# Second layer's feed forward over tokens sorted by routed expert: 17 blocks with one routed expert each, in place of 16 batches with both

## Chip, cores, metric

One core of one Trainium2 chip. The metric is the device time of one execution in microseconds (us). The kernel before takes 2658.98 us, the median of three runs (2656.93 to 2663.84).

## What is computed

Sixteen sequences of 256 tokens with 256 features go through two layers. Each layer is cross attention with 16 heads and then a feed forward, both added to the residual with a tanh gate. The change touches the feed forward of the second layer only:

```python
def _L1_ffn_ref(x, gate_w, w1, b1, w2, b2, sw1, sb1, sw2, sb2):
    xf = x.reshape(-1, D)                      # layer-normed tokens
    gate_scores = xf @ gate_w.T                # two routed experts
    top1 = jnp.argmax(softmax(gate_scores), axis=-1)
    one_hot = jax.nn.one_hot(top1, 2)
    masked = xf[None, :, :] * one_hot.T[:, :, None]
    h = relu(einsum('end,edh->enh', masked, w1) + b1[:, None, :])
    expert_out = einsum('enh,ehd->end', h, w2) + b2[:, None, :]
    shared = relu(xf @ sw1 + sb1) @ sw2 + sb2
    return expert_out.sum(axis=0) + shared     # hidden size 1024
```

An expert that is not chosen for a token still adds `relu(b1) @ w2 + b2`, the same vector for every token. All arithmetic is float32. Layer projections are made as three float32r products of high and low parts (`product3`).

## The kernel before

The program is written engine by engine; nothing schedules it. `layer0` is untouched by the change. `layer1` (from about 1357 us of the span) runs over batches of 256 tokens, two tiles of 128. Every engine has a function `body`, and one iteration of it is a software pipeline: batch `a` is in attention, batch `b = a - 1` in the feed forward, batch `c = a - 2` (on DVE) in its last sum, and `nxt = a + 1` has its first projections made. Inside, 20 steps `s` interleave the work of one head of attention with one piece of the feed forward. The order of each engine's instructions is fixed by this code, and engines wait for each other by semaphores.

Attention, per head and step: PE makes the scores of two heads (`pair_scores`, lines 1512 to 1524, even steps), DVE the row maximum (L1367), ACT the exponential (L1268), DVE the reciprocal (L1372), POOL the normalisation (L1157), PE the transposes (L1535, three steps later), DVE their copy (L1379), PE the product with the values (L1546 to L1549). The score tiles have two PSUM banks, so the pair of step `s + 2` starts when ACT has read both of step `s`. Projections of the own batch stand at steps 0 to 3 (v0, v1, k1, q1), of the next at 9, 14 and 16. After the steps PE makes `attn_out` (L1560) and DVE the residual (`attn_final`, L1385 and L1389).

Feed forward of batch `b`: DVE `ffn_norm` (L1299 to L1339) normalises, makes the two gate scores and `x0`, the tokens of expert 0 with the others zero; PE transposes `xf` and `x0` (L1488); ACT takes the high part, DVE the low (L1320); POOL makes `x1T = xfT - x0T` (L1172). Twelve hidden groups of 12 matmuls each follow, one per step at steps 0 to 11: four of the shared expert on `xfT`, four of expert 0 on `x0T`, four of expert 1 on `x1T`. ACT applies bias and relu (L1242). `ffn_down` (L1572) sums 24 chunks of hidden features for each token tile: tile 0 at the steps 16 to 19, tile 1 after `attn_out`. A float32 matmul of 128x256 counts as two instructions in the trace. DVE adds the biases (L1396) and the residual (L1403), and SP stores.

SP's loop (L1122) loads the input and the context of batch `b`, stores `b - 2`, and loads the residual of `b`. The load of the next batch waits only for `xn_ready` and `ctx_ready` of the batch before.

The weights of the feed forward are split into high and low parts once, in two pieces of 3072 columns, at steps 4 and 8 of iteration 0 (ACT L1206, DVE L1453). The head of DVE's body and the end of PE's:

```python
def body(a, b, c, nxt):
    if b is not None:
        ffn_norm(b)
    if c is not None:
        ffn_final(c)
...
def body(a, b, nxt):
...
    if a is not None:
        attn_out(a)
    if b is not None:
        for piece in range(4):
            ffn_down(b, 1, piece)
```

## Times and profile before

| | us |
|---|---|
| median of 3 runs | 2658.98 |
| lowest, highest | 2656.93, 2663.84 |
| the profiled execution's own time | 2655.57 |
| its span, first to last instruction | 2653.8 |
| PE busy | 2302.0 (87%) |
| DVE, ACT, POOL busy | 1493.3, 1267.8, 1022.9 |
| mean granted TensorE clock | 0.958 of 2.4 GHz |

The page gives the busy time of each engine over the span, slices, the chain that ended last, and the costliest groups of instructions. Matmuls overlap: one of 128x256 is shown as 280 to 380 ns long, while the next starts 117 ns later (float32r) or 216 ns later (one of the two instructions of a float32 product). So lengths of stretches are read from the starts, not from the sum of busy times.

### The profile page before, as it was taken

How to read it: one execution, taken by the hardware profiler on the slowest of the kernel's cores; microseconds unless marked ns; L12 is line 12 of the kernel's file. 1: busy time of each engine (PE TensorE's matmuls, PEld its weight loads, DVE VectorE, ACT ScalarE, POOL GpSimd, SP SyncE). 2: the span in 40 equal slices, each digit the busy share in tenths (PEclk: the TensorE clock that was granted, in tenths of full speed). 3: DMA queues.
4: the chain of work that ended last, by engine and by line, in shares of the span. 5: the costliest groups of instructions: out<-in, count | busy, mean ns of one | idle time of the engine just before them, and what ended most of it. 6: DMA issues, size and time to landing. Idle time of an engine off the chain costs nothing. (4 is left out here: it accounts for less than half of the span.)

```text
span 2653.8 us, 48232 instructions
## 1 busy us (share of the span) xinstructions
PE 2302.0 (87%) x16128; PEld 1929.3 (73%) x16128; DVE 1493.3 (56%) x3906; ACT 1267.8 (48%) x3971; POOL 1022.9 (39%) x910
## 2 busy tenths in 40 slices
PE   5888888888888888888456999999999999999998
PEld 4667777777777777776344777877777887777777
DVE  3467667676766776767645445444444544444441
ACT  5655566555556555556023444433344443334441
POOL 1355564555554555555512333221233322123320
PEclk8999999999989999999677999999999999999999
DMA  4000000000000000000040000000000000000000
GB/s 145 14 6 17 13 16 4 16 16 16 16 12 4 16 16 16 16 4 9 4 161 1 13 17 16 16 16 16 4 12 16 16 16 16 16 4 12 16 9 9
DMA packets 25856, 51.66 MB, mean 19 GB/s; under 512 B 6272, under 2 KB 7040, under 8 KB 24640
## 3 DMA queue, kind: packets, MB, share of 16 engines
q1 hardware_dynamic: 25792, 50.84, 5.7%
q8 instruction: 37, 0.61, 0.1%
q14 instruction: 27, 0.22, 0.0%
HBM read 42.44 MB, written 8.39 MB: 19 GB/s over the span
## 5 line engine op out<-in xcount | busy, mean ns | idle before, releaser
L1157 POOL TENSOR_SCALAR l_probs<-l_probs,l_rinv 128x256 f32<-128x256 f32 x512 | 238.9, 482 | 587.0 <-DVE l_rinv L1372 585.3
L1268 ACT ACTIVATE l_probs<-l_score,l_negmax 128x256 f32<-128x256 f32 x512 | 238.9, 473 | 264.6 <-DVE l_negmax L1367 264.6
L335 POOL TENSOR_TENSOR l_prod<-l_att,l_kv 128x2048 f32<-128x2048 f32 x64 | 288.3, 4545 | 181.2 <-DVE l_att L608 181.2
L321 POOL TENSOR_TENSOR l_prod<-l_q,l_kv 128x2048 f32<-128x2048 f32 x64 | 290.3, 4548 | 151.7 <-DVE l_att L591 80.8
L1572 PE MATMUL l_ffn<-l_w,l_hid 128*128 128x256 f32 x1536 | 347.1, 381 | 1.0 <-ACT l_hid L1242 1.0
L1572 PEld LDWEIGHTS l_ffn<-l_w,l_hid 128*128 128x128 f32 x1536 | 287.0, 190 | 50.1 <-issue 13.5
L1379 DVE COPY l_probsT<-l_attn 128x512 f32<-128x512 f32 x256 | 175.4, 685 | 157.6 <-PE l_attn L1535 157.3
L681 DVE CUSTOM_DVE_ANT_0 l_probs<-l_score,l_mbias 128x256 f32<-128x256 f32 (+1 forms) x512 | 161.2, 352 | 140.2 <-PE l_score L877 91.8
L1367 DVE TENSOR_REDUCE l_negmax<-l_score 128x2 f32<-128x512 f32 x256 | 174.9, 683 | 64.4 <-PE l_score L1523 64.4
L614 DVE TENSOR_REDUCE l_h<-l_prod 128x128 f32<-128x2048 f32 x64 | 146.3, 2286 | 103.4 <-POOL l_prod L335 102.4
L427 ACT COPY l_probsT<-l_attn 128x384 f32<-128x384 f32 x256 | 121.1, 473 | 143.8 <-PE l_attn L887 143.8
L410 ACT ACTIVATE l_probs<-l_probs,l_negmax 128x256 f32<-128x256 f32 x256 | 130.9, 511 | 104.4 <-DVE l_negmax L681 104.4
L110 PE MATMUL l_moe<-l_we_hi,l_h2T_hi 128*128 128x256 f32 x512 | 160.1, 313 | 12.4 <-DVE l_acc L665 10.7
L1242 ACT ACTIVATE l_hid<-l_ffn,l_b 128x256 f32<-128x256 f32 x384 | 161.5, 478 | 11.9 <-PE l_ffn L112 10.1
L1535 PE MATMUL l_attn<-l_ident,l_probs 128*128 128x128 f32 x1024 | 154.9, 277 | 9.4 <-DVE l_probsT L1379 7.3
L875 PE MATMUL l_score<-l_kT,l_qT 64*128 64x256 f32 x256 | 98.2, 467 | 61.2 <-DVE l_negmax L681 61.2
L110 PE MATMUL l_attn<-l_cT_hi,l_wk_hi 128*128 128x256 f32 x384 | 122.8, 320 | 31.8 <-DVE l_xT_lo L545 31.8
L591 DVE TENSOR_REDUCE l_att<-l_prod 128x128 f32<-128x2048 f32 x64 | 145.9, 2279 | 5.8 <-issue 3.9
L111 PE MATMUL l_moe<-l_we_lo,l_h2T_hi 128*128 128x256 f32 x512 | 147.9, 289 | 0.0
L112 PE MATMUL l_moe<-l_we_hi,l_h2T_lo 128*128 128x256 f32 x512 | 147.7, 289 | 0.0
L1535 PEld LDWEIGHTS l_attn<-l_ident,l_probs 128*128 128x128 f32 x1024 | 118.7, 142 | 23.6 <-issue 10.0
L665 DVE SCALAR_TENSOR_TENSOR l_acc<-l_moe,l_gate,l_acc 128x256 f32<-128x256 f32 x256 | 110.7, 474 | 40.8 <-PE l_moe L112 26.7
(273 smaller groups left out, 7441.9 us busy)
## 6 DMA issues: line engine op xcount, KB each, us to landing
l_ctxin<-in_ctx SPq DMA_DIRECT2D x32, 256.0 KB, 3.0
l_xin<-in_x SPq DMA_DIRECT2D x16, 256.0 KB, 2.7
l_x<-in_x SPq DMA_DIRECT2D x16, 256.0 KB, 2.6
x<-l_acc SPq DMA_DIRECT2D x16, 256.0 KB, 2.0
l_xin<-x SPq DMA_DIRECT2D x16, 256.0 KB, 3.3
l_x<-x SPq DMA_DIRECT2D x16, 256.0 KB, 2.7
out<-l_x SPq DMA_DIRECT2D x16, 256.0 KB, 2.0
l_hid<-in_w SPq DMA_DIRECT2D x2, 1536.0 KB, 9.7
```

What stands on the lines that cost most here:

```text
L110: last = nc.tensor.matmul(out, wh, xh, start=n == 0, stop=False)
L111: last = nc.tensor.matmul(out, wh, xl, start=False, stop=False)
L321: nc.gpsimd.tensor_tensor(prod[:, u].rearrange("p (h g d) -> p h g d", h=half, g=H), q4[:, u * half:(u + 1) * half].unsqueeze(2).to_broadc ...
L335: nc.gpsimd.tensor_tensor(prod[:, u].rearrange("p (h d g) -> p h d g", h=half, d=HD), a4.unsqueeze(2).to_broadcast([P, half, HD, H]), v4.u ...
L681: last = V.tensor_tensor_reduce(out=probs[:, j % 4, lo:hi], in0=ps[:, lo:hi], in1=mbias[:, lo:hi], scale=-HD0 ** -0.5, scalar=3e38, op0=AL ...
L1157: last = nc.gpsimd.tensor_scalar(probs[:, j % 4, t * S:(t + 1) * S], probs[:, j % 4, t * S:(t + 1) * S], rinv[:, j, t:t + 1], 1.0, ALU.mul ...
L1242: last = nc.scalar.activation(hid[:, c, :], ps[:, u * S:(u + 1) * S], ACT.Relu, bias=b1[:, c:c + 1])
L1268: last = nc.scalar.activation(probs[:, s % 4, t * S:(t + 1) * S], ps[:, t * S:(t + 1) * S], ACT.Exp, bias=negmax[:, s, t:t + 1], accum_out ...
L1367: V.tensor_reduce(negmax[:, j], ps[:].rearrange("p (t k) -> p t k", t=NT), axis=AX.X, op=ALU.max, negate=True).then_inc(max_ready, 1)
L1379: V.tensor_copy(probsT[:, j % 3, :], ps[:]).then_inc(free, 1)
L1535: last = T.transpose(ps[:, kt * S + t * P:kt * S + (t + 1) * P], probs[:, j % 4, t * S + kt * P:t * S + (kt + 1) * P], ident[:])
L1572: last = T.matmul(ps[:, 0:D], hid[:, c, t * P:(t + 1) * P], w2[:, c, :], start=c == 0, stop=c == 3 * NHC - 1)
```

## The change

The routed experts no longer see every batch. Each batch, after attention, is only routed: DVE makes the gate scores, PE ranks the tokens of expert 0 within the batch by a product with a triangle of ones, DVE forms for each token a place in the DRAM tensor `slots` (expert 0 from the front, expert 1 from the back), and POOL writes the 256 rows there by two indirect DMAs. A row holds the 256 features, the token's number, its mean and its reciprocal deviation. The feed forward then runs over 17 blocks of 256 rows of `slots`. Each block belongs to one routed expert, which DVE chooses from the counts (`choose`) and SP reads into registers. The weights of that expert come from DRAM for each block: the two split parts `e1` (1 MB each), the bias `be`, the second weights `e2` (1 MB), and `ce`, the constant of the expert not chosen. The output is written token by token, by two indirect DMAs of POOL for each block. A 17th block is needed because the places of the two experts need not end on a multiple of 256. Unused places are filled once with rows that go to rows of the output behind the last token.

A block has 8 hidden groups and 16 chunks in place of 12 and 24. The feed forward lags attention by three batches in place of one, so that three iterations have attention alone (0, 1, 2), thirteen have both (3 to 15), and four have the feed forward alone (blocks 13 to 16). Before it was one, fifteen and one.

```diff
+        hidden_at = {0: 0, 3: 1, 4: 2, 5: 3, 6: 4, 7: 5, 8: 6, 9: 7}
+        down_at = {10 + n: (2 * n, 2 * n + 2) for n in range(8)}
+        split_at = {4: 3, 8: 4, 14: 5}
-        ffn = Banks(nc, ctx, "l1_ffn", ["xfT", "x0T"] + [f"h{j}" for j in range(12)] + ["y0", "y1"])
+        ffn = Banks(nc, ctx, "l1_ffn", ["xfT"] + [f"h{j}" for j in range(8)] + ["y"])
...
@@ SP
+                def load_block(d):
+
+                    wait_apart(sp, sp_passed, choice_ready, d + 1)
+                    e = sp.value_load(choice[0:1, 0:1], min_val=0, max_val=1)
+                    n = sp.value_load(choice[0:1, 1:2], min_val=0, max_val=NBLOCK - 1)
...
+                        wait_apart(sp, sp_passed, scattered, 32 * (d + 2))
+                    if not first(d):
+                        wait_apart(sp, sp_passed, xe_copied, d)
+                    sp.dma_start(xe[:], slots.rearrange("(k t p) n -> k p t n", t=NT, p=P)[bass.ds(n, 1)][0]).then_inc(xe_in, 16)
...
+                        _, _, emptied, turn = ffn.at("h3", d - 1)
+                        wait_apart(sp, sp_passed, emptied, turn + 1)
+                    for part in range(2):
+                        sp.dma_start(flat(e1[part]).bitcast(F32), e1_parts[bass.ds(e, 1), part][0]).then_inc(e1_in, 16)
+                    sp.dma_start(be[:], ins["b1"][:, bass.ds(e * NHC + NHC, NHC)]).then_inc(e1_in, 16)
+                def load_second(d, e):
...
+                        wait_apart(sp, sp_passed, x4_ready, d)
+                    sp.dma_start(flat(e2), ins["w2"][:, bass.ds(e * (NHC * D) + NHC * D, NHC * D)]).then_inc(e2_in, 16)
+                    sp.dma_start(ce[:], ce_parts[bass.ds(e, 1)][0]).then_inc(e2_in, 16)
-                with sp.Fori(2, B) as b:
-                    load(b)
-                    store(b - 2)
-                    load_residual(b)
+                def body(i, d, nxt):
+                    if d is not None:
+                        e = load_block(d)
+                    if i is not None:
+                        load_residual(i)
+                    if nxt is not None:
+                        load(nxt)
+                    if d is not None:
+                        load_second(d, e)
+                with sp.Fori(3, B - 1) as i:
+                    body(i, i - 2, i + 1)
...
@@ POOL
+                def body(a, r, f, nxt):
+                    if f is not None and not first(f):
+                        store(f - 1)
+                    if r is not None:
+                        power(varF_ready, rstdF_ready, varF, rstdF, r)
                     for j in range(H):
...
+                        if r is not None and j == 3:
+                            scatter(r)
                         if nxt is not None and j == 5:
                             split_context(nxt)
...
@@ DVE
+                def place(r):
+                    dve.wait_ge(rank_ready, r + 1)
...
+                    V.tensor_tensor(count0[:], ranks[:, NT:NT + 1], count0[:], ALU.add).then_inc(rank_read, 1)
+                def other_expert():
+                    dve.wait_ge(split_lo, NS)
+                    V.tensor_scalar(b1[:, NHC:3 * NHC], b1[:, NHC:3 * NHC], 0.0, None, ALU.max)
+                    V.tensor_copy(hid[:, :, 0:P], b1[:, NHC:3 * NHC].unsqueeze(2).to_broadcast([P, 2 * NHC, P])).then_inc(relu_ready, 1)
+                    dve.wait_ge(other_full, 1)
...
+                def body(a, r, d, f, done, nxt):
+                    if r is not None:
+                        dve.drain()
+                        variance(x3, statF, mvF, varF, varF_ready)
+                    if done is not None:
+                        ffn_final(done)
+                    if f is not None:
+                        low(ffn, "xfT", f, xfT, xfT_hi)
+                    if r is not None:
+                        route(r)
                     for s in range(STEPS):
...
+                        if r is not None and s == 2:
+                            place(r)
+                        if d is not None and s == 2:
+                            choose(d)
...
+                        if d is not None and s == 15:
+                            block_normalise(d)
...
@@ PE
+                def rank(r, f):
+                    pe.wait_ge(wins_ready, r + 1)
+                    T.matmul(ps[:, 0:NT], above[:], first_wins[:], start=True, stop=False)
+                    T.matmul(ps[:, 1:NT], ones[:], first_wins[:, 0:1], start=False, stop=True)
+                    T.matmul(ps[:, NT:NT + 1], ones[:], first_wins[:, 0:1], start=True, stop=False)
+                    T.matmul(ps[:, NT:NT + 1], ones[:], first_wins[:, 1:2], start=False, stop=True).then_inc(rank_ready, 1)
+                def other_expert():
+                    pe.wait_ge(relu_ready, 1)
+                    pe.wait_ge(e2_raw_in, 32)
+                    for e in range(2):
+                        for c in range(NHC):
+                            last = T.matmul(ps[:, e * D:(e + 1) * D], hid[:, e * NHC + c, 0:P], (e2, w2)[e][:, c, :], start=c == 0, stop=c == NHC - 1)
                 def body(a, r, f, nxt):
...
+                        if r is not None and s == 2:
+                            rank(r, f)
+                        if f is not None:
+                            if s in hidden_at:
+                                if hidden_at[s] == 1 and r is not None:
+                                    pe.wait_ge(rank_read, r + 1)
+                                ffn_up(f, hidden_at[s])
+                            if s in down_at:
+                                ffn_down(f, 0, *down_at[s])
...
+                    if f is not None:
+                        ffn_down(f, 1, 0, 2 * NHC)
                     if a is not None:
                         attn_out(a)
-                    if b is not None:
-                        for piece in range(4):
-                            ffn_down(b, 1, piece)
```

In `store(f)` and `scatter(r)` POOL waits for `x4_ready` or `slot_ready` and issues one `indirect_dma_start` for each of the two tiles. The rank products go into the PSUM bank of the hidden group `h1`.

Three places of the order. First DVE, from the statistics of the batch that has left attention to the first row maximum of the next one. Before:

```order
L1304 TENSOR_SCALAR l_varF<-l_mvF 128x2
L1328 TENSOR_SCALAR l_xf<-l_x,l_mvF,l_rstdF 128x256 [waits l1_rstdF_ready]
...
L1336 TENSOR_TENSOR l_first_wins<-l_gscore 128x2
L1339 TENSOR_SCALAR l_x<-l_xf,l_first_wins 128x256 x2
...
L1396 TENSOR_TENSOR l_x<-l_ffn,l_b2sum 128x256 [waits l1_ffn1_full]
...
L1403 SCALAR_TENSOR_TENSOR l_x<-l_x,l_tg,l_x3res 128x512 [waits l1_x3_copied]
L1320 TENSOR_TENSOR l_xfT_lo<-l_ffn,l_xfT_hi 128x512 [waits l1_xfT_hi]
L1320 TENSOR_TENSOR l_x0T_lo<-l_ffn,l_x0T_hi 128x512 [waits l1_x0T_hi]
...
L1367 TENSOR_REDUCE l_negmax<-l_score 128x2 [waits l1_score0_full]
```

Now:

```order
L1409 TENSOR_SCALAR l_varF<-l_mvF 128x2
...
L1559 TENSOR_TENSOR l_x<-l_ffn,l_ce 128x512 [waits l1_stored]
L1563 CAST l_dest<-l_x3res 128x2 [waits l1_xe_copied]
L1564 SCALAR_TENSOR_TENSOR l_x<-l_x,l_tg,l_x3res 128x512
...
L1425 TENSOR_TENSOR l_xfT_lo<-l_ffn,l_xfT_hi 128x512 [waits l1_xfT_hi]
L1431 TENSOR_SCALAR l_xg<-l_row,l_mvF,l_rstdF 128x256 [waits l1_rstdF_ready]
...
L1442 TENSOR_TENSOR l_first_wins<-l_gscore 128x2
L1444 TENSOR_SCALAR l_other<-l_first_wins 128x2
L1446 TENSOR_TENSOR l_other<-l_other,l_down 128x2
...
L1527 TENSOR_REDUCE l_negmax<-l_score 128x2 [waits l1_score0_full]
```

The last sum of the feed forward (`ffn_final`) moved ahead of the gate scores, and the gate scores of the next batch now stand between the low part and the first maximum. Second, POOL at the head of the loop, now:

```order
L1265 DMA out<-l_x,l_dest 4352x256 [waits l1_x4_ready]
L1265 DMA out<-l_x,l_dest 4352x256
L1229 TENSOR_TENSOR l_rstdF<-l_varF,l_neghalf 128x2 [waits l1_varF_ready]
```

Before, the reciprocal deviation (`l_rstdF`, L1142) stood first and no store was POOL's. Third, SP's loop, now:

```order
L1137 DMA l_xe<-slots 128x2x260
...
L1145 ISA [waits l1_ffn0_free]
L1145 DMA l_e_hi<-e_parts 128x2048
...
L1145 DMA l_e_lo<-e_parts 128x2048
...
L1146 DMA l_be<-in_b 128x8
...
L1123 DMA l_row<-x 128x2x256
...
L1112 DMA l_xin<-x 128x512
L1115 DMA l_ctxin<-in_ctx 128x512 [waits l1_ctx_ready]
```

The loads of the next batch's input and context stand behind the wait for the fourth hidden group (`l1_ffn0_free`) and behind 2 MB of weights; before they stood at the head of the loop.

## Rows read from the trace of the kernel before

**Rows 1.** The page, costliest groups: ACT's exponential.

```profile
L1268 ACT ACTIVATE l_probs<-l_score,l_negmax 128x256 f32<-128x256 f32 x512 | 238.9, 473 | 264.6 <-DVE l_negmax L1367 264.6
```

**Rows 2.** Stretch, us; busy (count) PE, PEld, DVE, ACT, POOL; clock; DMA share; GB/s.

```profile
1372.00:1382.00 10.00, 5.83 (x38) 5.35 (x37) 4.90 (x11) 4.56 (x13) 0.00 (x0) 0.84 1.00 390
1379.00:1443.00 64.00, 41.21 (x272) 29.50 (x272) 35.35 (x68) 27.68 (x81) 17.43 (x35) 0.81 0.18 75
1444.00:1458.00 14.00, 8.27 (x40) 7.71 (x41) 6.88 (x24) 3.03 (x8) 0.70 (x1) 0.52 0.01 2
1597.00:1674.00 77.00, 72.66 (x520) 60.72 (x519) 36.23 (x90) 32.45 (x105) 21.11 (x39) 1.00 0.04 14
2598.00:2654.00 56.00, 49.48 (x297) 44.74 (x295) 9.58 (x27) 11.25 (x26) 3.84 (x4) 0.99 0.03 10
```

**Rows 3.** One line's instructions: the residual after attention; ns min/median/max, first and last start.

```profile
L1389 DVE SCALAR_TENSOR_TENSOR l_x<-l_ytmp,l_tg,l_x x16: 750/752/753, 1442.9 to 2598.9; 128x512 f32<-128x512 f32 x16
```

**Rows 4.** Timeline of PE, transposes and products: start us, us, engine, [idle before <-releaser].

```profile
1449.43 0.87 PE L1488 MATMUL l_ffn<-l_ident,l_xf 128*128 128x128 f32 x3 [7.30 <-DVE l_x L1339]
...
1670.08 3.69 PE L1560 MATMUL l_attn<-l_wo,l_oT 128*128 128x256 f32 x16 [0.76 <-issue]
...
2629.08 20.96 PE L1572 MATMUL l_ffn<-l_w,l_hid 128*128 128x256 f32 x96 [1.02 <-ACT l_hid L1242]
```

**Rows 5.** Timeline of ACT in the last feed forward: one hidden group.

```profile
2614.09 0.84 ACT L1242 ACTIVATE l_hid<-l_ffn,l_b 128x256 f32<-128x256 f32 x2 [0.56 <-PE l_ffn L112]
```

**Rows 6.** Timeline of DVE, end of one iteration and head of the next.

```profile
1676.67 0.17 DVE L1304 TENSOR_SCALAR l_varF<-l_mvF 128x2 f32<-128x2 f32 x1
1677.65 0.73 DVE L1328 TENSOR_SCALAR l_xf<-l_x,l_mvF,l_rstdF 128x256 f32<-128x256 f32 x2 [0.82 <-POOL l_rstdF L1142]
...
1680.05 0.16 DVE L1336 TENSOR_TENSOR l_first_wins<-l_gscore 128x2 f32<-128x2 f32 x1
...
1684.75 0.75 DVE L1403 SCALAR_TENSOR_TENSOR l_x<-l_x,l_tg,l_x3res 128x512 f32<-128x512 f32 x1 [0.16 <-issue]
1685.42 0.68 DVE L1320 TENSOR_TENSOR l_xfT_lo<-l_ffn,l_xfT_hi 128x512 fp32r<-128x512 f32 x1
...
1686.62 0.68 DVE L1367 TENSOR_REDUCE l_negmax<-l_score 128x2 f32<-128x512 f32 x1
```

**Rows 7.** Timeline of PE, head of the next iteration.

```profile
1683.97 0.60 PE L1488 MATMUL l_ffn<-l_ident,l_xf 128*128 128x128 f32 x4
...
1686.81 0.36 PE L110 MATMUL l_ffn<-l_xfT_hi,l_w_hi 128*128 128x256 f32 x1 [0.84 <-DVE l_x0T_lo L1320]
...
1691.43 0.35 PE L1521 MATMUL l_score<-l_k_hi,l_q 32*128 32x256 f32 x1
```

**Rows 8.** Timeline of POOL: reciprocal deviation, context split, normalisation.

```profile
1676.92 0.70 POOL L1142 TENSOR_TENSOR l_rstdF<-l_varF,l_neghalf 128x2 f32<-128x2 f32 x1 [20.18 <-DVE l_varF L1304]
...
1630.30 0.63 POOL L1149 CAST l_cT_hi<-l_ctxin 128x512 fp32r<-128x512 f32 x1
1631.09 1.28 POOL L1151 TENSOR_TENSOR l_cT_lo<-l_ctxin,l_cT_hi 128x512 fp32r<-128x512 f32 x1 [0.15 <-issue]
1632.35 0.93 POOL L1157 TENSOR_SCALAR l_probs<-l_probs,l_rinv 128x256 f32<-128x256 f32 x2
```

**Rows 9.** Timeline of DVE, steps 2, 3 and 7 of a full iteration.

```profile
1618.77 0.87 DVE L1347 SCALAR_TENSOR_TENSOR l_k_lo<-l_attn,l_bk,l_k_hi 128x256 fp32r<-128x256 f32 x2 [3.12 <-ACT l_k_hi L1230]
...
1633.07 0.74 DVE L1299 BATCH_NORM_STATS2 l_statC<-l_xin 128x6 f32<-128x256 f32 x2
```

**Rows 10.** Timeline of PE, scores of steps 2 and 4 in that iteration.

```profile
1614.14 0.35 PE L1521 MATMUL l_score<-l_k_hi,l_q 32*128 32x256 f32 x1
...
1621.44 0.35 PE L1521 MATMUL l_score<-l_k_hi,l_q 32*128 32x256 f32 x1
```

**Rows 11.** Timeline of SP: the next batch's input is asked for.

```profile
1618.22 0.33 SPq L1091 DMA_DIRECT2D l_xin<-x  x1
```

**Rows 12.** Timeline of DVE, a weight split in iteration 0.

```profile
1396.28 3.36 DVE L1453 TENSOR_TENSOR l_w_lo<-l_hid,l_w_hi 128x3072 fp32r<-128x3072 f32 x1 [3.07 <-ACT l_w_hi L1206]
```

More of the change, by code:

```diff
@@ L1096, in load_residual @@
                 def load_residual(b):
-                    if not first(b):
-                        sp.wait_ge(x3_copied, b)
-                        sp.wait_ge(xf_ready, b)
-                    sp.dma_start(x3[:], x2[bass.ds(b, 1)][0]).then_inc(xres_in, 16)
-                def store(b):
-                    sp.wait_ge(x4_ready, b + 1)
-                    sp.dma_start(out[bass.ds(b, 1)][0], x4[:]).then_inc(x4_stored, 16)
+                    if first(b):
+                        sp.wait_ge(gap_stored, 32)
+                    else:
+                        sp.wait_ge(scattered, 32 * b)
```

376 lines of the change are left out of this document (244 added, 132 removed).

## Prediction

> **What bounds the kernel now.** I read the busy time by stretch first. In a full iteration of the second layer PE has 72.66 us of records in 77, DVE 36.23, ACT 32.45, POOL 21.11, and the DMA engines move 14 GB/s at a share of 0.04 [rows 2]. So PE bounds it, at full clock. The residual after attention starts sixteen times between 1442.9 and 2598.9 us [rows 3], one iteration per 77.07 us, and 54.9 us follow the last. Second, what may take PE's place: an iteration with attention alone. Iteration 0 is one. From its first scores to its end, 64 us, PE has 41.21 us and the granted clock averages 0.81 [rows 2]. Heads pass in turn through DVE, ACT, POOL and PE, and less work on PE doesn't shorten that round. So less feed forward is worth what a full iteration loses until that round binds, less what the new iterations cost.
>
> **What PE loses.** A hidden group passes every 1.40 us (ACT's 0.84 and the 0.56 before it, waiting for PE) [rows 5]: four fewer, 5.6 us. The last feed forward's 96 instructions take 20.96 us, 0.437 for each of 48 float32 products [rows 4]: 16 fewer, 7.0. One set of transposes fewer, 0.6 [rows 7]; the rank products add some 0.5 (an estimate from the cheapest groups here). Net 12.7 us per iteration. POOL loses the two subtractions of `other_tokens`, as long as the 1.28 of the context's [rows 8], DVE a low part of 0.68 [rows 6]; neither engine bounds.
>
> **The head of an iteration.** Call T the end of the output product, near 1673.6 in the rows [rows 4]. Before, DVE's first maximum starts at 1686.62, T + 13.0 [rows 6], but PE fills this with the second half of `ffn_down`, 24 products or 10.4 us, and transposes. Now that half stands ahead of the output product and covers nothing. DVE's chain: variance done at 1676.84, T + 3.2 [rows 6]; then the last sum and residual, two passes of 0.68 and 0.75 with 0.2 between, so `x4_ready` at T + 5.0; low part to T + 5.7. POOL waits for `x4_ready`, issues two indirect DMAs and only then makes the reciprocal deviation, 0.70 [rows 8]. No row shows an indirect DMA. Bounds for one: 0.33, what SP needs to issue a DMA [rows 11], and 4.5, some three and a half of POOL's 1.28 us passes over 128x512 [rows 8], since it handles 128 rows one by one. I take 1.2, near POOL's pass over such a tile. The deviation is then there at T + 8.3. From there to the gate's comparison it is 2.40 (1677.65 to 1680.05) [rows 6], and three copies and three small operations with drains make 1.0. First maximum at T + 11.7. The next pair of scores needs maximum 0.68, two exponentials of two passes of 0.473 [rows 1], relu 0.84 between them [rows 5], hand-overs: 3.6. The scores of step 2 start at T + 15.3; before at 1691.43, T + 17.8 [rows 7]. PE has 4 us of work in this stretch, so of 10.4 + 0.6 + 1.4 us that left it, only 2.5 are gained.
>
> The Trainium skill, "DMA: Bandwidth & Descriptors", section "Anatomy of one DMA — SWDGE (gpsimd) path", gives about 2.0 us plus bytes / 436e9 per DMA from GpSimd, most of it the receipt and not the issue. By it two DMAs would be done 2.3 us after issue, and if POOL were held as long for each, the head would be 2.2 us longer than in my sum. No row here shows which.
>
> **Steps 2 to 4.** Before, 1614.14 to 1621.44: 7.3 us with two hidden groups in it [rows 10]. Now `h1` waits for `rank_read`. DVE gives it in `place`, which stands behind the low part of k1, and that waits 3.12 us for ACT behind PE's k1 projection [rows 9]. Scores, rank and k1 take PE 2.7; ACT 0.9; DVE's low part 0.87 [rows 9]; `place` 0.5: PE stands some 2.4 us. Then come two more operations of `place` and eight of `choose`, 0.16 each with five drains, 1.8, ahead of the maximum of step 3; 0.68 and an exponential of 1.0 later step 4 can score: 8.8 us. The queue behind also makes the next maximum 0.6 late.
>
> **Steps 4 to 10.** SP asks for the next batch's input at 1618.22 now, 15 us before DVE's use at 1633.07 [rows 9, 11]. After the change it does so behind the wait for the fourth hidden group, step 5, whose relu ends near T + 31, and behind 2 MB of `e1` and two smaller loads. At the 390 GB/s that the start of the layer reached [rows 2] 2 MB take 5.4 us, the 0.75 MB with them 2.0, landing and issues 2: the input is there at T + 40, the context a little later. DVE wants the one at step 7, T + 36; POOL the other after head 5 and needs 2.0 us with it before it can normalise head 6 [rows 8]. I take 4 us of stall; bounds 0 (loads that share the queue and finish early) and 7. The rest stays as in the trace of the same iteration, read off the starts of the scores: 11.8 us for steps 4 to 8 and 7.1 for 8 to 10.
>
> **Steps 10 to the end.** With less beside them steps 10 to 12 fall to 4.4 and 12 to 14 rise to 4.6, since a pair with no feed forward beside it takes 4.1 (steps 12 to 14 of that iteration). From step 14 to T: 23.6 before; 8.7 us of products go and 6.9 of the other tile come, transposes of the last heads wait for q0's copy on DVE: 23.8.
>
> Sum: 15.3 + 8.8 + 0.6 + 11.8 + 11.1 + 4.4 + 4.6 + 23.8 = **80.4 us per full iteration, against 77.1**.
>
> **The whole.** Iteration 0: three splits of 2048 columns for two of 3072, 3.36 us of DVE each after 3.07 of waiting for ACT [rows 12], the same in sum; the last waits for stores of 2 MB behind 4.5 MB of gap rows and 2 MB of loads, and POOL's constants come first: +5 (0 to 15). `other_expert` between iterations 0 and 1: copy of 2048 columns 2.2, 16 products of 0.437 7.0, sums and hand-overs 1.8: +11, hidden by nothing. Iterations 1 and 2: iteration 0 without its two splits (62.9 − 12.8 = 50), head 7.5 more, `place` and `choose` 2.5: 60 each. Iteration 3 has no last sum and no store yet: 76. Twelve full ones 964.8, the last without a next batch, −3. So the last residual after attention is at 1442.9 + 5 + 11 + 120 + 76 + 964.8 − 3 = 2616.7. Then block 13: T + 32 (low part 5.7, eight groups 11.2, relu 1.0, 32 products 14.0); blocks 14 to 16: 11.2 + 1.0 + 14.0 and 3.0 of sum, transposes and low part, 29.2 each, their weights landing beneath; last sum, stores, landing 6.5. 125 us, where 54.9 stood. The span ends at 2741.8; its own time is 1.8 over the span, 2743.6, and the median lies 3.4 over the profiled execution: **2747 us**. Slower by 88, of which 13 × 3.3 is in the full iterations and the rest is unpaired work at both ends.
>
> **Rivals.** (1) *PE stays the bound.* If the round of heads has slack that I count as stall (the input lands in time, `place` overlaps, the head costs 6 us of idle PE), a full iteration takes PE's 77.1 − 12.7 plus 6, near 70. Then 2747 − 13 × 10.4 = 2612: faster. For it: the trace shows waits of only 4 us per iteration, and DVE at 36 of 77. Against: iteration 0 shows PE idle a third of its time with no feed forward. The sign turns at 73.6 us per full iteration, (2747 − 2659) / 13 below mine. (2) *The clock falls.* After PE stood 7.30 us [rows 4] the granted clock was 0.52 over 14 us [rows 2], near the 1.2 GHz level. Each iteration now has stands of some 4.5, 6.5 and 2.4 us. If half clock covers k1, `h1`, q1 and transposes, 4 us per iteration come on top: 2800. (3) *POOL's stores are dear.* At 3 us for an indirect DMA the head grows 3.6, twelve times: 2790. DVE's chain runs while POOL issues them. The Trainium skill, "SBUF — State Buffer", section "SBUF: two separate sides", says that DVE's two-port passes lock GpSimd out of writing descriptors; by that rule this rival comes about through DVE's passes, and no row here has a DMA of POOL to show it. (4) *Only the loads are no stall*: 2747 − 52 = 2695, still slower. That the blocks don't shrink can be left out: the order of instructions has eight groups.
>
> **Chances.** Mine with its spread (2690 to 2770) 0.52; rivals 2 and 3, alone or together, 0.22; rival 1 0.22; near the turning point 0.04. Two runs of one kernel differ by 0.3%, which I take as what can be told from no change. So faster 0.22, same 0.03, slower 0.75. The range reaches from 2640, which leaves out most of rival 1, to 2815, which takes in rivals 2 and 3.
>
> **What would show it.** Right: residuals after attention some 80 us apart from batch 4 on; POOL's indirect DMAs directly ahead of `l_rstdF`, which DVE waits for; PE waiting at step 2 for ACT, at step 3 for DVE's `l_count`; `l_statC` waiting for the DMA of `l_xin`; four blocks of 29 us at the end. Wrong: a period under 73.6, or a clock of 1.00 with PE over 90% busy.

## The result, and the profile after

The changed kernel takes 2917.84 us (median of four runs, 2917.30 to 2918.24); four runs of the kernel before gave a median of 2658.20. The ratio is 1.0972, with a 95% interval from 1.0953 to 1.0991. It is slower, as forecast, but by 260 us and not by 88, and it lies above the range.

The page of the changed kernel. TensorE's clock over 40 slices drops where the second layer starts and stays lower until the tail:

```profile
span 2915.9 us, 46926 instructions
...
PE 2276.5 (78%) x15108; PEld 1892.6 (65%) x15108; DVE 1533.7 (53%) x4182; ACT 1220.8 (42%) x3845; POOL 1055.4 (36%) x957
...
PEclk9999999999999999976786888888888888888899
```

In the kernel before, the same row falls below 8 in three slices only and is at 9 behind them:

```profile
PEclk8999999999989999999677999999999999999999
```

PE's share of the span fell from 87% to 78%, and in the full iteration below PE has 69 us of records in 91, where it had 72.66 in 77: the bound has gone from PE to waits. The residual after attention, which answers to [rows 3]:

```profile
L1549 DVE SCALAR_TENSOR_TENSOR l_row<-l_ytmp,l_tg,l_row x16: 750/752/752, 1453.3 to 2777.3; 128x512 f32<-128x512 f32 x16
```

By the single starts of this line, iteration 0 ends 10.4 us later than before; iterations 1 and 2 take 76.0 and 77.2 us (the first holds `other_expert`), iteration 3 takes 86.9, the eleven full ones with a next batch average 91.5 (1007.0 in sum), and the last, without one, 76.9. Then 138.6 us follow to the end of the span.

One full iteration by stretches (columns as in [rows 2]): about the head, steps 2 to 4 and the rest, and below them the end of the kernel.

```profile
2059.00:2074.00 15.00, 5.66 (x35) 5.11 (x33) 9.70 (x32) 2.83 (x10) 3.60 (x5) 0.71 0.29 96
2074.00:2089.00 15.00, 11.93 (x56) 11.34 (x56) 4.60 (x19) 4.04 (x14) 2.54 (x6) 0.50 0.00 0
2089.00:2150.00 61.00, 51.76 (x352) 40.82 (x352) 24.31 (x54) 22.06 (x73) 16.78 (x31) 0.94 0.15 56
...
2780.00:2916.00 136.00, 112.19 (x660) 103.32 (x660) 18.69 (x69) 28.67 (x67) 14.96 (x17) 0.92 0.28 99
```

PE is busy 5.7 of 15 us at the head. Then the granted clock is 0.50, the 1.2 GHz level, for a stretch in which the instructions look busy only because each takes longer.

In that iteration the output product ends at T = 2058.65 (the residual starts 1.07 later, here and below). PE's stands at the head, in its timeline, and the scores of step 4:

```profile
2064.87 0.55 PE L114 MATMUL l_ffn<-l_xfT_hi,l_e_hi 128*128 128x256 f32 x1 [4.95 <-DVE l_xfT_lo L1425]
...
2074.57 0.55 PE L1693 MATMUL l_score<-l_k_hi,l_q 32*128 32x256 f32 x1 [4.96 <-ACT l_probs L1371]
...
2082.85 0.58 PE L114 MATMUL l_ffn<-l_xfT_hi,l_e_hi 128*128 128x256 f32 x1 [2.50 <-DVE l_count L1458]
...
2089.12 0.39 PE L1693 MATMUL l_score<-l_k_hi,l_q 32*128 32x256 f32 x1
```

The stands are those of the forecast: 4.95 for the low part (forecast 4.5), 4.96 for the exponentials (6.5), 2.50 for the ranks (2.4). The same head on POOL, with its scatter and the context of the next batch:

```profile
2064.64 1.11 POOL L1265 DMA_INDIRECT out<-l_x,l_dest  x1 [22.17 <-DVE l_x L1564]
2066.05 0.96 POOL L1265 DMA_INDIRECT out<-l_x,l_dest  x1 [0.30 <-issue]
2067.04 0.72 POOL L1229 TENSOR_TENSOR l_rstdF<-l_varF,l_neghalf 128x2 f32<-128x2 f32 x1
...
2093.56 1.10 POOL L1252 DMA_INDIRECT slots<-l_row,l_slot  x1 [0.17 <-issue]
...
2108.44 0.61 POOL L1236 CAST l_cT_hi<-l_ctxin 128x512 fp32r<-128x512 f32 x1 [10.64 <-DMA l_ctxin<-in_ctx]
```

DVE, three places: the deviation that stands behind the stores; in step 4 the maximum of head 4 and the reciprocal of head 3, for which POOL's scatter waits; and the next batch's input, where [rows 9] showed no wait:

```profile
2067.80 0.73 DVE L1431 TENSOR_SCALAR l_xg<-l_row,l_mvF,l_rstdF 128x256 f32<-128x256 f32 x2 [3.17 <-POOL l_rstdF L1229]
...
2091.50 0.68 DVE L1527 TENSOR_REDUCE l_negmax<-l_score 128x2 f32<-128x512 f32 x1
2092.10 0.15 DVE L1532 RECIPROCAL l_rinv<-l_rsum 128x2 f32<-128x2 f32 x1
...
2107.66 0.75 DVE L1404 BATCH_NORM_STATS2 l_statC<-l_xin 128x6 f32<-128x256 f32 x2 [7.17 <-DMA l_xin<-x]
```

SP's queue says why the input is late. It answers to [rows 11]:

```profile
2097.78 0.39 SPq L1137 DMA_DIRECT2D l_xe<-slots  x1
2098.53 0.34 SPq L1145 DMA_DIRECT2D l_e_hi<-e_parts  x1
2099.05 0.33 SPq L1145 DMA_DIRECT2D l_e_lo<-e_parts  x1
2099.59 0.33 SPq L1146 DMA_DIRECT2D l_be<-in_b  x1
2100.10 0.57 SPq L1123 DMA_DIRECT2D l_row<-x  x1
2100.91 0.41 SPq L1112 DMA_DIRECT2D l_xin<-x  x1
```

SP stands until `scattered` lets `xe` go, 1.9 us behind POOL's scatter (2094.96 and 0.96 more). All that follows on its queue is issued in one burst, and the input comes last but one: asked for at T + 42.3, there at T + 49.0, wanted at T + 41.8. ACT's relu of the fourth hidden group, h3, had ended at T + 37.0. The context lands with the input, and PE's next transposes wait for POOL, which splits it first. From ACT's timeline and PE's:

```profile
2094.75 0.87 ACT L1346 ACTIVATE l_hid<-l_ffn,l_be 128x256 f32<-128x256 f32 x2
```

```profile
2111.77 1.12 PE L1707 MATMUL l_attn<-l_ident,l_probs 128*128 128x128 f32 x4 [6.97 <-POOL l_probs L1244]
```

Behind that stand the granted clock is 0.56 for the 5.3 us up to the scores of step 10.

Where a full iteration went, read off the starts of the scores:

| part of a full iteration | forecast | changed kernel |
|---|---|---|
| T to the scores of step 2 | 15.3 | 15.9 |
| steps 2 to 4 | 8.8 | 14.6 |
| 4 to 8 | 12.4 | 11.5 |
| 8 to 10 | 11.1 | 16.45 |
| 10 to 14 | 9.0 | 9.8 |
| 14 to T | 23.8 | 23.5 |
| sum | 80.4 | 91.8 |

Two parts miss, by 5.8 and by 5.35 us. Both differ between iterations: over the eleven full ones steps 2 to 4 take 13.2 to 14.6 us (mean 13.7) and steps 8 to 10 take 15.8 to 18.2 (mean 17.2), so by the means they miss by 4.9 and 6.1. The other parts are the same in all of them within 0.3 us. The experiments take these two apart, and then the head.

### The profile page after: what moved, and what is told of

Its sections match the earlier page's. It is cut to its first block, busy times and chain, and to the rows that moved or that the text cites. A ratio compares the mean times of both kernels' runs of the same rounds, so it can differ in the third digit from the quotient of the medians.

```text
span 2915.9 us, 46926 instructions
## 1 busy us (share of the span) xinstructions
PE 2276.5 (78%) x15108; PEld 1892.6 (65%) x15108; DVE 1533.7 (53%) x4182; ACT 1220.8 (42%) x3845; POOL 1055.4 (36%) x957
## 4 chain that ended last, share of the span: by engine, by line
PE 24%; issue 7%; DVE 7%; DMA 5%; ACT 5%; POOL 2%; DVEq 1%; SPq 1%; POOLq 0%; ACTq 0%
PE l_ffn L1751 7%; DMA l_ctxin<-in_ctx 3%; PE l_attn L1707 2%; PE l_attn L1732 2%; ACT l_probs L1371 2%; DVE l_negmax L1527 2%; PE l_attn L114 2%; PE l_attn L116 1%; PE l_attn L115 1%; PE l_ffn L114 1%; DMA slots<-l_row,l_slot 1%; PE l_heads L1718 1%; PE l_ffn L115 1%; PE l_ffn L116 1%; PE l_score L1693 1%
## 5 line engine op out<-in xcount | busy, mean ns | idle before, releaser
L1707 PE MATMUL l_attn<-l_ident,l_probs 128*128 128x128 f32 x1024 | 174.0, 299 | 128.9 <-POOL l_probs L1244 108.6
L1707 PEld LDWEIGHTS l_attn<-l_ident,l_probs 128*128 128x128 f32 x1024 | 132.4, 153 | 156.9 <-POOL l_probs L1244 95.7
L114 PE MATMUL l_ffn<-l_xfT_hi,l_e_hi 128*128 128x256 f32 x272 | 99.7, 366 | 106.2 <-DVE l_xfT_lo L1425 73.2
L1265 POOL DMA_INDIRECT out<-l_x,l_dest x34 | 34.6, 1017 | 400.7 <-DVE l_x L1564 367.4
L114 PE MATMUL l_moe<-l_we_hi,l_h2T_hi 128*128 128x256 f32 x512 | 158.0, 309 | 12.4 <-DVE l_acc L669 10.7
L1693 PE MATMUL l_score<-l_k_hi,l_q 32*128 32x256 f32 x256 | 84.8, 348 | 104.5 <-ACT l_probs L1371 101.9
L114 PE MATMUL l_attn<-l_cT_hi,l_wk_hi 128*128 128x256 f32 x384 | 141.0, 367 | 30.5 <-DVE l_xT_lo L549 30.5
L1693 PEld LDWEIGHTS l_score<-l_k_hi,l_q 32*128 32x128 f32 x256 | 51.9, 203 | 145.6 <-issue 140.6
```

The source lines that it names most:

```text
L114: last = nc.tensor.matmul(out, wh, xh, start=n == 0, stop=False)
L1693: T.matmul(ps0[:, out], q[r0, c, m], k[0][r0, c, :], start=True, stop=False)
L1707: last = T.transpose(ps[:, kt * S + t * P:kt * S + (t + 1) * P], probs[:, j % 4, t * S + kt * P:t * S + (kt + 1) * P], ident[:])
```

## The experiments

Every ratio is to runs of the kernel before on the same chip. Experiments 7, 8, 10 and 11 ran on another chip than the rest; the kernel before took 2659.18 us there and 2656.65 to 2657.08 here. "Period" is the distance of residuals in full iterations. Where steps are given as a mean, it is that of the eleven full iterations.

**1. Loads ahead of the block's loads.**

```diff
 def body(i, d, nxt):            # SP
+    if nxt is not None:
+        load(nxt)
     if d is not None:
         e = load_block(d)
     if i is not None:
         load_residual(i)
-    if nxt is not None:
-        load(nxt)
```

> SP asks for the next batch's input and context ahead of the wait for the choice, the wait for the scatter and the 2 MB of e1. Theory (order on SP): in the changed kernel DVE stands 7.2 us for l_xin and steps 8 to 10 last 16.45 us against 7.1 before, so some 9 us come back in each of the eleven full iterations with a next batch and in iterations 1 to 3: full iteration 91.8 to about 83, the whole 2918 to about 2790. Rival (the DMA engines are what is short, or the next wait in line is POOL's normalised heads for another reason): x_in lands early but the residuals stay 89 to 92 us apart, the whole 2880 to 2918.

2785.85 us, ratio 1.0494 [1.0476, 1.0512]. The period is 82.0, iterations 2 and 3 take 62.0 and 76.6, and steps 8 to 10 take 7.08 us as before the change. POOL's context split has no wait left:

```profile
2110.69 0.60 POOL L1236 CAST l_cT_hi<-l_ctxin 128x512 fp32r<-128x512 f32 x1
```

The wait is gone and the expectation (about 2790) holds. So the order on SP's queue cost 132 us, half of the loss. 62.0 and 76.6 are also what the forecast had for such iterations (60 and 76).

**2. The last sum ahead of the output product.** DVE does `ffn_final(f)` at the end of its body, not at the head of the next.

```diff
 # DVE body, head
-    if done is not None:
-        ffn_final(done)
 # DVE body, end
+    if f is not None:
+        ffn_final(f)
     if a is not None:
         attn_final(a)
```

> The last sum of the feed forward (bank y is full before the output product starts) is done on DVE ahead of attn_final, at the end of the body, so x4_ready and POOL's two stores come some 4 us earlier and the head of the next iteration is attn_final, variance, low part, gate. Theory (the head is a serial chain on DVE and POOL): first maximum from T + 12.4 to about T + 8.3, some 4 us less in each of 13 iterations: about 2864; if the shorter stand also keeps the clock up, 2800 to 2830. Rival (the head hides behind something else, for instance the scores of step 2 wait for ACT): first maximum earlier, residuals still 91 us apart, 2905 to 2918.

2843.54 us, ratio 1.0697 [1.0657, 1.0736]. From the scores of step 0 to those of step 2 it is 10.3 us in place of 15.4. Steps 2 to 4 take 11.1 to 14.2, mean 12.7 in place of 13.7. Periods are 82 to 88, since the loads still stop steps 8 to 10 (mean 17.0 us). The time lies between the two that were expected (2864, and 2800 to 2830 with the clock up): 5 us per iteration are the head's, 1 is of steps 2 to 4. The chain of DVE and POOL does set the head.

**3. Ranks in step 4.** `rank` on PE, `place` and `choose` on DVE move from step 2 to step 4, into the bank of `h2`; the scatter from head 3 to head 5.

```diff
-    if r is not None and s == 2:
+    if r is not None and s == 4:
         rank(r, f)
...
-    if r is not None and j == 3:
+    if r is not None and j == 5:
         scatter(r)
```

> The rank products, place and choose move from step 2 to step 4 and into the bank of the third hidden group, ahead of the copy of transposes on DVE; the scatter moves from head 3 to head 5. Theory (place stands behind k1 and stops PE for 2.5 us, choose delays the maximum of step 3 by 1.8): 3 to 4 us less per iteration over 14 iterations, about 2870. Rival (the wait only moves two steps on, and the scatter, and with it the loads behind it on SP, comes later): 0 to +4 us per iteration, 2918 to 2970.

2976.91 us, ratio 1.1202 [1.1183, 1.1220]: slower by 59 us. In the means steps 2 to 4 fall from 13.7 to 7.8, 4 to 6 rise from 5.9 to 11.7, and 8 to 10 rise from 17.2 to 21.5. The last is the loss. In an iteration where it is larger than most (23.4 us), in DVE's timeline (T = 1990.6):

```profile
2045.28 0.75 DVE L1404 BATCH_NORM_STATS2 l_statC<-l_xin 128x6 f32<-128x256 f32 x2 [13.62 <-DMA l_xin<-x]
```

The scatter starts at T + 38.4, not at T + 34.9, and the input lands at T + 54.7. SP asks for `xe` 1.9 us behind the scatter here too, and 6.4 us behind the end of h3's relu. So it is the scatter that SP's loads wait for, and not h3's relu as forecast.

**4. PE kept busy at the head.**

```diff
+def keep_busy(banks, use, batch, n):
+    ps, _, free, turn = banks.at(use, batch)
+    pe.wait_ge(free, turn)
+    for _ in range(n):
+        T.matmul(ps[:, 0:S], wk[0][:, 0, 0:P], cT[0][:, 0, :], start=True, stop=True)
...
+    keep_busy(attn, "v0", a, 32)   # ahead of h0
...
+    keep_busy(ffn, "h1", f, 32)    # ahead of the scores of step 2
```

> PE gets useless work in its two stands at the head of each full iteration: 32 products of 256 columns into the bank of v0 ahead of the first hidden group, 32 into the bank of h1 ahead of the scores of step 2 (3.4 us each at the full clock, in stands of 4.95 and 4.96 us). No wait is taken away. Theory (the half clock after the stands costs): granted clock between T + 15 and T + 30 rises from 0.50 towards 1, steps 2 to 4 fall from 14.5 to about 10 us, 4 to 5 us less per full iteration, about 2855. Rival (that stretch is bound by the waits on DVE and ACT, the clock costs nothing, or the clock does not react to such work): within 10 us of 2918, or up to 2960 if the products run at half clock and push what is behind them.

2903.71 us, ratio 1.0937 [1.0917, 1.0957], 14 us under the changed kernel: neither the 2855 of the theory nor within 10 us of 2918 as by its rival. Steps 2 to 4 take 11.1 to 14.2, mean 12.9 in place of 13.7. The stands were not closed: in the iteration below the clock is 1.00 in the first 15 us but falls again behind a stand of 2.89 us that was left ahead of step 2, and steps 2 to 4 take 14.2:

```profile
2141.00:2156.00 15.00, 11.37 (x96) 10.86 (x96) 9.37 (x32) 3.11 (x11) 3.74 (x5) 1.00 0.28 96
2156.00:2171.00 15.00, 12.27 (x64) 11.55 (x64) 4.60 (x19) 4.17 (x15) 2.43 (x5) 0.54 0.00 0
```

**5. The same with both stands closed, on the kernel of experiment 1.** 38 and 54 products in place of 32 and 32.

> Loads first, with useless products as before but enough to close both stands of PE at the head: 38 ahead of the first hidden group, 54 ahead of the scores of step 2 (32 and 32 left stands of 0.98 and 2.89 us, and the clock fell to 0.54 after the second). Against the run with the loads first alone (residuals 81.9 apart, steps 2 to 4 14.1 us at a granted clock of 0.56). Theory (the half clock of steps 2 to 4 comes from these stands and costs 4 to 5 us): clock near 1 in steps 2 to 4, which take 9 to 10 us; residuals 77 to 78 apart; about 2730. Rival A (the clock falls after the stand of 2.50 us for the ranks, or whatever PE does): 0.5 to 0.6 again, 14.1 us, about 2760 to 2790. Rival B (full clock, but the waits on DVE bind there): clock 1, 12 us or more, 2765 to 2790.

2742.96 us, ratio 1.0334 [1.0317, 1.0351], 43 us under experiment 1 with more work in it. The period is 78.5 in place of 82.0, a little over the 77 to 78 that were expected. PE's timeline (L1800 is the useless product) and the two stretches:

```profile
2062.64 0.36 PE L114 MATMUL l_ffn<-l_xfT_hi,l_e_hi 128*128 128x256 f32 x1 [0.26 <-DVE l_xfT_lo L1425]
2065.53 6.55 PE L1800 MATMUL l_ffn<-l_cT_hi,l_wk_hi 128*128 128x256 f32 x54
2072.33 0.35 PE L1693 MATMUL l_score<-l_k_hi,l_q 32*128 32x256 f32 x1 [0.24 <-ACT l_probs L1371]
2078.07 0.58 PE L114 MATMUL l_ffn<-l_xfT_hi,l_e_hi 128*128 128x256 f32 x1 [2.50 <-DVE l_count L1458]
```

```profile
2056.00:2071.00 15.00, 14.74 (x124) 14.16 (x123) 9.74 (x32) 2.06 (x7) 2.84 (x4) 1.00 0.39 131
2071.00:2083.00 12.00, 9.26 (x66) 8.68 (x64) 4.70 (x20) 4.80 (x17) 3.31 (x7) 0.86 0.00 0
```

Steps 0 to 2 take 15.4 us as without the useless work, so the clock costs nothing there. Steps 2 to 4 take 10.76 in place of 14.1, and they do so in each of the eleven iterations within 0.1 us: the clock is worth 3.35 us of them. It is not at full speed even so (0.86). The stand for the ranks is 2.50 as before, and the first hidden group behind it runs slowly again (0.58 for the product's first instruction).

**6. POOL's stores behind the deviation, on experiment 1.**

```diff
-    if f is not None and not first(f):
-        store(f - 1)
     if r is not None:
         power(varF_ready, rstdF_ready, varF, rstdF, r)
+    if f is not None and not first(f):
+        store(f - 1)
```

> Loads first, and POOL issues its two stores behind the reciprocal deviation and not ahead of it. Theory (each indirect DMA holds POOL for 1.0 to 1.1 us, and the deviation waits behind two of them and behind the last sum): the deviation is made at about T + 4.1 and is there before DVE's low part ends; DVE's stand of 3.16 us goes, the first maximum comes 3 us earlier: residuals 79 apart, about 2786 - 14 x 3 = 2744. Rival (DVE stands for something else as long, or the stores, now later, hold up POOL's first normalised head): 81 to 82 apart, 2770 to 2790.

2722.30 us, ratio 1.0249 [1.0224, 1.0275], 64 us under experiment 1. Period 75.9 to 78.1. T is 2047.63 here, in POOL's timeline, DVE's and PE's:

```profile
2051.11 0.70 POOL L1229 TENSOR_TENSOR l_rstdF<-l_varF,l_neghalf 128x2 f32<-128x2 f32 x1 [19.61 <-DVE l_varF L1409]
```

```profile
2053.57 0.73 DVE L1431 TENSOR_SCALAR l_xg<-l_row,l_mvF,l_rstdF 128x256 f32<-128x256 f32 x2
...
2057.01 0.69 DVE L1527 TENSOR_REDUCE l_negmax<-l_score 128x2 f32<-128x512 f32 x1
```

```profile
2060.55 0.35 PE L1693 MATMUL l_score<-l_k_hi,l_q 32*128 32x256 f32 x1 [1.22 <-ACT l_probs L1371]
```

The stand of 3.17 is gone, the first maximum starts at T + 9.4 in place of 12.4, and PE's second stand is 1.22 us. The expectation had 3 us of it and the run shows 5: steps 2 to 4 take 11.1 to 13.3, mean 12.1 in place of 14.1. They are short where the granted clock is higher (11.1 us at 0.69, 12.7 at 0.60, against 14.1 at 0.52 in experiment 1), so part of the clock came back with the shorter stand.

**7. Loads first and the last sum early, together.**

> Loads first and the last sum ahead of the output product, together. If the two causes are separate (loads 9.8 us, head 6.2 us per full iteration, as each showed alone), residuals come some 76 us apart (82.0 less 6) and the whole is 2786 less 14 x 5.5, about 2710. If they overlap (the earlier head only lengthens a later wait once the loads are in time), residuals stay at 79 to 82 and the whole at 2750 to 2786.

2709.11 us, ratio 1.0168 [1.0143, 1.0194], period 76.1 in the mean. The two causes add up: alone they gave 132 and 74 us, together 209.

**8. The same with the ranks in step 4.**

> The same, with the rank products, place and choose in step 4. Alone that move cost 4 us per iteration. Theory (it cost because the later scatter held the loads back on SP): with the loads first it gains instead, 1 to 3 us per iteration, 2670 to 2700. Rival (the later place itself costs, by stopping PE at step 4 as it did at step 2 or by the half clock): 2 to 4 us per iteration more than the run without it, 2740 to 2770.

2707.43 us, ratio 1.0178 [1.0161, 1.0195]: the same as without, within what runs differ. With the loads in time steps 2 to 6 take 18.6 us in place of 19.3 in the mean, and the period falls by the same 0.7 (74.3 to 76.3, mean 75.4). Iterations 1 and 2 take 7 us more than in experiment 7, which uses that up. Neither the gain of 1 to 3 us per iteration nor the rival's loss of 2 to 4 came. What experiment 3 lost was lost through the loads: behind the same move steps 8 to 10 take 7.2 us here and 21.5 there.

**9. The kernel before, with the second half of the last product ahead of the output product.**

```diff
-    if a is not None:
-        attn_out(a)
     if b is not None:
         for piece in range(4):
             ffn_down(b, 1, piece)
+    if a is not None:
+        attn_out(a)
```

> The kernel before, with one thing of the change: PE does the second half of the feed forward's last product ahead of the attention's output product. Theory (that half covers the head of the iteration, and the change took the cover away): the scores of step 2 stay about 14 to 18 us behind the end of the output product while 10.4 us of PE's work no longer lie in them, so 8 to 12 us more per iteration over 15 iterations, with the clock down at the head: 2780 to 2840. Rival (the chain of the head in the kernel before is long only because its last sum waits for that half, and shortens when the half is early): 0 to 4 us more per iteration, 2655 to 2720.

2793.27 us, ratio 1.0519 [1.0501, 1.0536]. The period is 85.7 to 87.0 against 77.3. First 15 us from about T + 1 in the kernel before, then the same in this one:

```profile
2061.50:2076.50 15.00, 14.08 (x85) 12.34 (x85) 8.36 (x26) 3.04 (x8) 0.70 (x1) 1.00 0.05 17
```

```profile
2051.00:2066.00 15.00, 8.67 (x47) 8.08 (x48) 8.71 (x27) 3.31 (x9) 0.74 (x2) 0.66 0.05 17
```

One exchange of two products on PE costs 137 us in a kernel that has nothing else of the change: PE is busy 8.67 of 15 us in place of 14.08, and the clock falls to 0.66. The first maximum starts at T + 10.7 here, against T + 13.0 in [rows 6], but little of that arrives: the scores of step 2 start 17.1 us behind T in the mean, against 17.65. From step 14 to T it is 33.4 us in place of 23.8, so of the 9.6 us that now lie ahead of T only 0.6 is won back behind it.

**10. The half behind the output product again, on experiment 1.** PE as in the kernel before; DVE does gate, last sum, low part, in this order; POOL's stores behind the deviation.

```diff
     if a is not None:
         attn_out(a)
+    if f is not None:
+        ffn_down(f, 1, 0, 2 * NHC)
```

> Loads first; PE does the last feed forward's second half behind the output product again, as the kernel before did, POOL issues its stores behind the reciprocal deviation, and DVE makes route, then the last sum, then the low part. Theory (that half is what covered the head before): 7 us of PE's work lie beside 9 us of DVE's chain, no stand over 4 us, the clock stays near 1: the scores of step 2 start some 8 us of PE's work earlier in the sum, residuals 73 to 77 us apart, about 2690. Rival (h0 and the first maximum now wait for the last sum, which waits for that half, so the chain only starts later): residuals 80 to 82 apart, 2760 to 2790.

2689.36 us, ratio 1.0109 [1.0092, 1.0126], period 73.5 to 75.2. The theory holds for the period. Its clause on the clock doesn't. PE's stands at the head are 2.15 and 1.75 us, and yet the granted clock is 0.52 in the steps 2 to 4 behind them, which take 14.2 us in that iteration and 12.9 in the mean. The time is 33 us under experiment 6 (37 by the ratios). DVE's order changed along with PE's, so what the cover alone is worth is not shown.

**11. The half behind the scores of heads 0 and 1, on experiment 1.** Now the exponentials run beside it too. The main lines of the edit:

```diff
-hidden_at = {0: 0, 3: 1, ...
+hidden_at = {2: 0, 3: 1, ...
 # PE body, s == 0, behind pair_scores(a, 0)
+    if done is not None and s == 0:
+        ffn_down(done, 1, 0, 2 * NHC)
 # DVE body, head
+    low(ffn, "xfT", f, xfT, xfT_hi)
+    attn_max(a, 0)
+    attn_max(a, 1)
     route(r)
     ffn_final(done)
 # POOL body
     power(varF_ready, rstdF_ready, varF, rstdF, r)
 # behind head 2
+    store(f - 1)
+    copy_residual(f)
```

> Loads first; PE: output product, transposes of the next block, scores of heads 0 and 1, then that second half, v0, v1, scores of step 2, rank, first hidden group (moved from step 0 to step 2); DVE: variance, low part, both first maxima, gate, last sum; place ahead of q1 and k1's low parts where its step allows; POOL: deviation first, stores and residual copy behind head 2. By the sum PE has no stand over 3 us at the head: scores of step 2 at about T + 11 of which 9 us are PE's own work, clock near 1.00, residuals 68 to 72 us apart: 2785 less 14 x 12, about 2620, faster than the kernel before. Rival (DVE's chain of 9 us and place still stop PE as long, only elsewhere): residuals 76 to 80 apart, 2700 to 2760.

2556.62 us, ratio 0.9610 [0.9594, 0.9626]: faster than the kernel before by 3.9%, and 361 us faster than the changed kernel, with the same operations in another order, and 63 us under the expectation. The period is 65.8. Orders on SP, PE, DVE and POOL changed together; their shares were not taken apart, other than that of the loads in experiment 12. Its page, and the two stretches (T is 2038.35):

```profile
PE 2163.6 (85%) x15108; PEld 1797.9 (70%) x15108; DVE 1527.6 (60%) x4182; ACT 1220.8 (48%) x3845; POOL 1060.4 (41%) x957
```

```profile
2038.00:2048.00 10.00, 10.00 (x59) 8.69 (x57) 8.23 (x29) 2.52 (x9) 0.70 (x1) 1.00 0.00 0
2048.00:2058.00 10.00, 8.59 (x76) 8.00 (x75) 5.68 (x23) 4.21 (x14) 2.98 (x7) 1.00 0.48 170
2058.00:2105.00 47.00, 44.29 (x324) 35.21 (x320) 24.80 (x55) 22.24 (x74) 19.67 (x34) 0.96 0.18 67
```

The columns are those of [rows 2]. The scores of step 2 start at T + 9.7 and PE has worked all the time until then. Steps 2 to 4 take 9.6 us at full clock. PE is the bound again, at the shorter work that the change was to give it.

**12. The order of experiment 11 with the changed kernel's order on SP.**

> The order with the second half behind the scores of heads 0 and 1, without the loads first: the changed kernel's order on SP. If the causes add up, 9.8 us per iteration come back over it: residuals 75 to 76 apart, about 2556 + 130 = 2690. Rival (with a shorter head the loads are asked for earlier too, so that the stall shrinks): it is SP's wait for the scatter and for h3's relu that starts them, both earlier now by some 10 us from T, but so are steps 7 to 8 that use the input: the stall stays. If only DVE's use moved less than the loads, residuals 70 to 73, 2620 to 2660.

2699.12 us, ratio 1.0167 [1.0150, 1.0184], period 74.6 to 77.6: the loads cost 142 us here too, 9.9 us per full iteration, and the statistics wait 6.87 us for the input. A better head doesn't hide them. Here h3's relu and the scatter's issue end within 0.1 us of each other, so this run doesn't tell the two apart.

## Why the prediction was right in direction and wrong in size

**What PE loses, and what covers the head.** Right. PE's 12.7 us didn't shorten the iteration, because the half that moved ahead of the output product was the cover of DVE's and POOL's chain. Experiment 9 shows it in the kernel before; 10 and 11, which changed other orders as well, fit it in the changed one. T to the scores of step 2 was forecast at 15.3 us and took 15.9: the deviation was there at T + 9.1 (8.3), the first maximum at T + 12.4 (11.7).

**Steps 2 to 4: the term that was mis-sized.** 8.8 us forecast, 14.6 measured in that iteration and 13.7 in the mean. The stand was right, but I costed PE's work at full clock and left the half clock to rival 2. The traces had shown both halves of it: 7.30 us of idle PE [rows 4] and a clock of 0.52 in the 14 us behind [rows 2]. With three forecast stands of 4.5, 6.5 and 2.4 us the full clock was the unlikelier case. In experiment 1 the same steps take 14.1, 5.3 over the forecast. Experiment 5 shows 3.35 of the 5.3 us to be the clock's, where rival 2 had 4; the other 2 us, with the slow group behind the ranks' stand in them, weren't taken apart. The terms that the forecast writes out for its 8.8 add up to 8.45; the 0.35 between has no source.

**Steps 4 to 10: the wrong wait, and a stall of 4 us that was 9 to 10.** 4 us of stall forecast, 9.4 measured in that iteration (16.45 less the 7.08 of experiment 1), 10.0 by the means. The mechanism was named, the load of the next batch behind `e1` on SP, but I took h3's relu at T + 31 as what releases SP. Two things failed in that. The relu itself ended at T + 37.0, most of the delay being that of the slow steps 2 to 4, which I hadn't carried on. And SP was released later still, by the scatter, which I had in no sum. It stands on POOL behind head 3, whose reciprocal DVE makes in step 4 only, behind the low part of q1 and the maximum of head 4. So it starts at T + 34.9, `xe` is asked for at T + 39.1 and `e1` at T + 39.9. From there to the landing of the input it is 9.1 us, as forecast (9). The input is there at T + 49.0 where I had T + 40; DVE's use had moved from T + 36 to T + 41.8, so DVE waits 7.17 us in place of 4. What PE feels is POOL's wait for the context: PE stands 6.97 us, and the products behind that stand run at a granted clock of 0.56 and take 2.1 us more than in experiment 1, together 9.1 of the 9.4. So the half clock cost here too, which neither my case nor rival 2 had. Experiment 1 shows that the order on SP is the cause, experiment 3 that the scatter is what SP waits for, and experiment 12 that the loss stays with a short head.

**The whole.** The last residual came at 2777.3, 160.6 behind my 2616.7: 5.4 in iteration 0 (inside its bounds, not taken apart), 22.2 in iterations 1 and 2, 10.9 in iteration 3, 122.6 in the eleven full ones, −0.5 in the last. Iterations 1 to 3 missed by the loads: I had no stall in them, and with the loads first they take 72.4, 62.0 and 76.6 against my 71, 60 and 76. The tail was 138.6 us, 13.5 over the forecast. I let block 13 end at T + 32 as if it ran alone, but the gate and the ranks of the last batch stand in it. From PE's timeline (the output product ended at 2776.3):

```profile
2781.97 0.58 PE L114 MATMUL l_ffn<-l_xfT_hi,l_e_hi 128*128 128x256 f32 x1 [5.06 <-DVE l_xfT_lo L1425]
2788.50 0.35 PE L1764 MATMUL l_ffn<-l_first_wins,l_above 128*128 128x2 f32 x2 [3.61 <-DVE l_other L1444]
```

The block's products end at T + 41.8. The granted clock is 0.81 to 0.85 until `ffn_down` starts, which is part of it. The other 4 us lie behind it: blocks 14 to 16 take 29.1, 31.0 and 30.7 us in place of 29.2, and the end 7.0 in place of 6.5.

**The rivals.** *PE stays the bound*: not in this kernel, but its arithmetic was near: experiment 11 has a period of 65.8, below the 70 of that rival, and it is faster than before. That it got there by another order of the same work was not in the rival. *The clock falls*: true, beside my case and not in place of it. *POOL's stores are dear*: wrong by their own duration. They issue in 0.96 to 1.11 us (forecast 1.2), but they stood in a bad place, and moving them behind the deviation gave 64 us. *The loads are no stall*: wrong; they are the largest single part, 132 us. I set rival 2 as a chance against my case, when it came on top of it, and by experiment 3 whatever delays the scatter delays the loads. My range ended at 2815 because it allowed one rival at a time, on top of a stall of 4 us whose upper bound I had at 7, when it was 9 to 10.

## What to carry to other kernels

Work that is taken from the bounding engine, or put in another order on it, is worth what still lies beside the serial chains: before it is removed, list which chain each piece covers, and place the large free pieces where the next operation has just been given to the other engines. A load that nothing holds back belongs ahead of every wait in its queue; behind a wait it inherits the lateness of all that the wait depends on. When a forecast contains stands of TensorE, cost the stretch behind them at both clock levels, and put the lower one into the sum if the trace of before shows it after such a stand; here two stands of 2.15 and 1.75 us were followed by it (experiment 10).

## What the runs showed of the hardware

POOL's indirect DMA of 128 rows, which no row before showed. Durations on POOL in ns, minimum, median, maximum, and the times to landing in us, first for the scatter, then for the stores:

```profile
L1252 POOL DMA_INDIRECT slots<-l_row,l_slot x32: 956/1011/1236, 1486.3 to 2792.5; - x32
...
DMA to landing us min/median/max: 2.4/2.6/3.5
```

```profile
L1265 POOL DMA_INDIRECT out<-l_x,l_dest x34: 957/962/1110, 1698.5 to 2912.6; - x34
...
DMA to landing us min/median/max: 2.4/4.5/5.3
```

The two stores of a block at the head run beside the 1 MB of `e2` that the same sum releases. All 32 stores for which SP had issued that load 0.6 to 2.3 us earlier land after 3.9 to 5.3 us; the last two, with no load beside them, land after 2.4. The Trainium skill, "DMA: Bandwidth & Descriptors", section "Anatomy of one DMA — SWDGE (gpsimd) path", puts most of such a DMA in the receipt and not in the issue. The rows agree in part: POOL is free after 1.0 us and the data are there after 2.4 to 2.6, so the larger part lies behind the issue, but the issue is not small.

The Trainium skill, "SBUF — State Buffer", section "SBUF: two separate sides", says that passes of DVE can lock GpSimd out of writing descriptors. On POOL no price of it shows: no scatter took over 1.24 us to issue, and in experiment 6 the stores, issued beside DVE's gate, took 1.11 and 1.03. On DVE one does show: two of its small copies (L1433 and L1434, 128x2) take 0.16 us in the changed kernel, and 0.43 and 0.37 us in the median of the 13 iterations of experiment 6 in which a store is issued beside them.

The clock at the head costs only what is bound by PE there. Useless products that closed stands of 4.95 and 4.24 us left steps 0 to 2 at 15.4 us and took 3.35 off steps 2 to 4. A stand of 2.89 us left open was followed by a clock of 0.54 in experiment 4, and stands of 2.15 and 1.75 us by 0.52 in experiment 10. In experiment 11 a stand of 1.42 us ahead of step 4 left the clock at 1.00 before it and 0.96 in the stretch behind.
